# Expert weights split inside layer 0's loop, the experts' first norm on ScalarE, and the ranking behind an expert block

## The reference

```python
x = x + windowed_attention(group_norm(x))      # layer 0: 12 heads of 8, shifted 8x8 windows, q and k normalised
t = tokens(x)
t = t + local_attention(layer_norm(t))         # layer 1: 6 heads of 16, causal, 16 tokens back
scores = layer_norm(t) @ gate_w + gate_b       # 4 experts
probs  = softmax(scores); keep the top 2, divide by their sum
h = gelu(n @ w1[e] + b1[e])                    # 96 -> 384, n = layer_norm(t)
y = h @ w2[e] + b2[e]                          # 384 -> 96
t = t + sum over experts of gate[e] * y[e]
```

## Time and profile before

| | us |
|---|---|
| median of 3 runs (lowest, highest) | 498.88 (495.75, 503.75) |
| the profiled execution's own time | 497.59 |
| its span, first to last instruction | 493.5 |
| PE busy | 433.9 (88%) |
| DVE busy | 362.0 (73%) |
| ACT busy | 335.1 (68%) |
| POOL busy | 131.6 (27%) |

### The profile page before, as it was taken

The page is one execution under the profiler, slowest core; times in us unless marked ns, Lnnn a source line. Parts: engine busy times, 40 slices in busy tenths (PEclk is TensorE's granted clock), DMA queues, the critical chain, the costliest instruction groups (busy, mean ns, idle before and its releaser), DMA issues.

```text
span 493.5 us, 14736 instructions
## 1 busy us (share of the span) xinstructions
PE 433.9 (88%) x5354; PEld 324.2 (66%) x5354; DVE 362.0 (73%) x1056; ACT 335.1 (68%) x898; POOL 131.6 (27%) x257
## 2 busy tenths in 40 slices
PE   2547999999999996889999999788998999999995
PEld 1114767777776765667777777566885677777773
DVE  4976778787888788457767777647677777777776
ACT  1016787777778785268888888555777777777773
POOL 8302222222121226033433334553912000000000
PEclk9999999999999999589999999997999999999998
DMA  7112000000000000000000000000500232212300
GB/s 174 23 30 71 28 8 0 0 0 1 0 0 0 0 0 2 1 2 3 3 0 0 0 0 0 2 1 1 129 2 17 68 81 80 57 25 80 80 14 18
DMA packets 14326, 12.36 MB, mean 25 GB/s; under 512 B 12803, under 2 KB 13143, under 8 KB 13528
## 3 DMA queue, kind: packets, MB, share of 16 engines
q1 hardware_dynamic: 13128, 11.74, 9.3%
q10 hardware_dynamic: 1072, 0.08, 0.2%
q0 software_dynamic: 96, 0.14, 0.1%
HBM read 10.31 MB, written 1.70 MB: 24 GB/s over the span
## 4 chain that ended last, share of the span: by engine, by line
PE 65%; ACT 10%; DVE 10%; SPq 6%; issue 4%; DMA 2%; POOL 1%; DVEq 0%; ACTq 0%
PE bank L651 8%; PE bank L663 6%; PE score_banks L718 5%; PE score_banks L1283 4%; PE score_banks L1280 4%; PE score_banks L1281 4%; PE bank L684 3%; PE bank L708 3%; PE bank L590 3%; PE score_banks L1269 3%; PE score_banks L625 3%; PE score_banks L1270 3%; ACT probsT L816 3%; PE score_banks L1271 3%; PE score_banks L606 2%
## 5 line engine op out<-in xcount | busy, mean ns | idle before, releaser
L985 POOL TENSOR_TENSOR stack<-qk,ones 128x192 f16<-128x192 f32 x64 | 32.4, 506 | 183.2 <-DVE qk L907 115.4
L1432 DVE TENSOR_TENSOR hidden_lo<-hidden,hidden_hi 128x512 fp32r<-128x512 f32 x96 | 65.6, 685 | 20.1 <-ACT hidden_hi L1336 20.0
L839 DVE TENSOR_REDUCE negmax<-score_banks 128x12 bf16<-128x768 f32 (+1 forms) x64 | 48.2, 754 | 25.7 <-PE score_banks L625 25.7
L651 PEld LDWEIGHTS bank<-vals,probsT 128*64 128x64 f32 (+1 forms) x1536 | 36.9, 127 | 29.0 <-ACT probsT L813 19.1
L651 PE MATMUL bank<-vals,probsT 128*64 128x18 f32 (+1 forms) x1536 | 42.5, 208 | 13.9 <-ACT probsT L816 4.5
L1334 ACT ACTIVATE hidden<-score_banks 128x512 f32<-128x512 f32 x64 | 38.3, 598 | 21.7 <-PE score_banks L1271 17.7
L718 PE MATMUL score_banks<-perm,probs 128*128 128x128 f32 x288 | 43.9, 281 | 0.7 <-ACT probs L786 0.7
L663 PE MATMUL bank<-w_qkv,xnT 128*128 128x192 f32 x128 | 40.2, 398 | 3.9 <-DVE qk L907 3.0
L1280 PE MATMUL score_banks<-hidden_hi,w_hi 128*96 128x512 f32 x96 | 38.6, 402 | 2.2 <-ACT hidden_hi L1336 2.2
L1283 PE MATMUL score_banks<-hidden_lo,w_hi 128*96 128x512 f32 x96 | 38.5, 401 | 1.7 <-DVE hidden_lo L1432 1.7
L813 ACT ACTIVATE probsT<-score_banks 128x384 f32<-128x384 f32 x32 | 15.7, 490 | 34.4 <-PE score_banks L718 34.4
(11 more groups left out here) (195 smaller groups left out, 1105.5 us busy)
## 6 DMA issues: line engine op xcount, KB each, us to landing
xT_all<-gate_scratch SPq DMA_DIRECT2D x8, 768.0 KB, 5.2
x_all<-in_x SPq DMA_DIRECT2D x4, 384.0 KB, 7.3
out<-moe_final SPq DMA_DIRECT2D x8, 192.0 KB, 2.2
w<-in_w SPq DMA_DIRECT2D x1, 582.0 KB
w<-in_w SPq DMA_DIRECT2D x1, 576.0 KB
bias_f<-col_scratch SPq DMA_DIRECT2D x16, 24.0 KB
perm<-in_permutations SPq DMA_DIRECT2D x1, 320.0 KB, 3.2
w_qkv<-in_w_qkv SPq DMA_DIRECT2D x2, 109.1 KB
```

The lines of the kernel that those rows point to most:

```text
L651: last = pe.matmul(o_bank[rows, pair_of[h2] * 2 * vd:(pair_of[h2] + 1) * 2 * vd], probsT[:, h2, rows], buffer_of(k, odd, -1)[:, w, pair_of ...
L839: v.tensor_reduce(negmax[:].rearrange("p (g h) -> p g h", g=2), score_banks[k][:, :, 0:half].rearrange("p g (h j) -> p g h j", j=KEYS), AX ...
L1432: v.tensor_tensor(hidden_lo[m % HBUF][:], hidden[m % 2][:], hidden_hi[m % HBUF][:], ALU.subtract).then_inc(q["hidden_lo"], 1)
```

## The change

Four edits. First, w2_hi is made by ACT, between steps 2 and 3 of layer 0, behind a wait for `experts_loaded` at 64; POOL makes w1_lo and w2_lo in 24 slices each (64 and 48 columns wide), one pair at the end of each step of layer 0's loop; POOL's block of three operations after the loop is gone. Second, the guess of the experts' norm, part 0, is taken by ACT, between layer 1's loop and step N - 4, in place of POOL. Third, `dve_gates(0)` stands ahead of DVE's step N (the last division), no longer behind it, and `rank_first` stands in chunk 0, block 0, behind `dve_low`. Fourth, the statistics of part 1 move from ahead of the expert stage to chunk 0, block 2, behind `dve_low`; POOL's power of part 1 still waits for them.

```diff
@@ gpsimd
-            middle_steps(pool, a0["pool"])
+            pool.wait_ge(w1_split, 1)
+            pool.wait_ge(w2_split, 1)
+
+            def pool_middle(pool, b, k, odd):
+                a0["pool"](pool, b, k, odd)
+                split_weights(nc, s, q0, 2 * b + k)
+
+            middle_steps(pool, pool_middle)
             steps(pool, a0["pool"], N - 4, N - 2)
-            pool.wait_ge(w1_split, 1)
-            nc.gpsimd.tensor_tensor(s["w1_lo"][:], s["w1"][:], s["w1_hi"][:], ALU.subtract).then_inc(w1_split, 1)
-            pool.wait_ge(w1_split, 2)
-            pool.wait_ge(s["experts_loaded"], 16 * 4)
-            split_second_weights(pool, nc, s, q0["w2_split"])
+            pool.wait_ge(w1_split, 1 + MIDDLE)
+            pool.wait_ge(w2_split, 1 + MIDDLE)
             steps(pool, a1["pool"], -3, 4)
             middle_steps(pool, a1["pool"])
-            norm_power(pool, nc, s, qm, 0)
@@ vector
-            steps(v, a1["dve"], N, N + 1)
             moe["dve_gates"](v, 0)
-            moe["dve_rank"](v)
-            steps(v, a1["dve"], N + 1, N + 3)
-            norm_statistics(v, s, qm, 1, q1["stat_ready"])
-            moe["dve"](v)
+            steps(v, a1["dve"], N, N + 3)
+            moe["dve"](v, lambda: norm_statistics(v, s, qm, 1, q1["stat_ready"]))
@@ scalar
-            steps(act, a0["act"], 0, 4)
+            steps(act, a0["act"], 0, 3)
+            act.wait_ge(s["experts_loaded"], 16 * 4)
+            nc.scalar.activation(s["w2_hi"][:], s["w2"][:], ACT.Copy).then_inc(w2_split, 1)
+            steps(act, a0["act"], 3, 4)
             act.wait_ge(s["w1_loaded"], 16)
             nc.scalar.activation(s["w1_hi"][:], s["w1"][:], ACT.Copy).then_inc(w1_split, 1)
...
             middle_steps(act, a1["act"])
+            norm_guess(act, nc, s, qm, 0)
             steps(act, a1["act"], N - 4, N - 2)
+MIDDLE = UNITS - 8
+SLICE1, SLICE2 = EXPERTS * HID // MIDDLE, NH * C // MIDDLE
+
+def split_weights(nc, s, q, n):
+    one, two = bass.ds(SLICE1 * (n - 4), SLICE1), bass.ds(SLICE2 * (n - 4), SLICE2)
+    flat, hi, lo = (s[w][:].rearrange("p m c -> p (m c)") for w in ("w2", "w2_hi", "w2_lo"))
+    nc.gpsimd.tensor_tensor(s["w1_lo"][:, one], s["w1"][:, one], s["w1_hi"][:, one],
+                            ALU.subtract).then_inc(q["w1_split"], 1)
+    nc.gpsimd.tensor_tensor(lo[:, two], flat[:, two], hi[:, two], ALU.subtract).then_inc(q["w2_split"], 1)
@@ dve_chunk
             if is_chunk(c, 0):
                 if m == 0:
+                    rank_first(v)
                     dve_select(v, 0)
                     dve_renormalise(v, 0)
                 if m == 1:
                     dve_gates_T(v, 0)
+                if m == 2:
+                    last_statistics()
```

More of the change, by code:

```diff
@@ L1017, in whole_program @@
     N = UNITS
-    w1_split = q0["w1_split"]
+    w1_split, w2_split = q0["w1_split"], q0["w2_split"]
     with nc.Block() as block:
@@ L1464, in weigh_at, with dve_chunk @@
         return m // HC - 1 if m % HC == 1 and m > 1 else None
-    def dve_chunk(v, c, k):
+    def dve_chunk(v, c, k, last_statistics=None):
         for m in range(NH):
@@ L1559, in sync_program, with dve_program @@
             sp.wait_ge(stored[k], 16 * (CHUNKS // 2))
-    def dve_program(v):
-        chunks(v, dve_chunk)
+    def dve_program(v, last_statistics):
+        chunks(v, lambda v, c, k: dve_chunk(v, c, k, last_statistics))
         c, k = CHUNKS - 1, 1
@@ L1593, in experts @@
             "pe": pe_program, "pe_inputs": pe_inputs, "act_inputs": act_inputs, "dve_inputs": dve_inputs,
-            "pe_gates": pe_gates, "dve_gates": dve_gates, "dve_rank": rank_first,
+            "pe_gates": pe_gates, "dve_gates": dve_gates,
             "normalise": normalise_first}
```

## The result

The changed kernel takes 500.36 us (median of 20 runs, 496.65 to 502.37); the kernel before, run beside it, 497.01 (20 runs, 493.74 to 505.1). The ratio is 1.0072, 95% interval 1.0047 to 1.0097: a small loss, where a small gain was forecast. The profiled execution is the fastest of its 20: span 494.6, own time 496.65, mean granted clock 0.975 (before 493.5, 497.59, 0.969). It is 3.7 us under the kernel's median, while the profiled execution of the kernel before is 0.6 over the median of 497.01. So what follows takes places from the traces and the verdict from the timed runs; 4.3 us of what separates the two medians and the two profiled times is in neither trace.

What follows compares the result with a forecast made beforehand. PE was taken to set the pace in layer 0's loop, with stalls and half clock behind them at three places. Terms -8.5 + 0 + 7.0 - 3.3 + 1.2 = -3.6 gave 495.3 us; 8-in-10 range 487.5 to 503.5.

Steps and rivals of the forecast that it cites:

- Rival B: Layer 0 from 66 us: long half clock behind ACT's wait, 13.5 in place of 7, 501.8 us; chance 0.14.
- rival C: End of layer 0: clock falls all the same, gain 4 in place of 8.5, 499.8 us; chance 0.15.
- POOL's block at the end of layer 0: Removing it frees DVE's L962 and avoids PE's wait and half clock: -8.5 us, bounds 3 and 9.5.
- E: End of layer 0: DVE held by something other than POOL's block, no gain there, 503.8 us; chance 0.02.
- Slices: Layer 0's loop: they fall beside DVE's row maximum and cost 0 us, bounds 0 and 9.6.
- D: Layer 0's loop: slices catch DVE's root each step, +9.6 us, 504.9 us; chance 0.04.
- ScalarE's copy and wait: Ahead of layer 0's step 3: PE delayed 5.5 us, plus 1.7 of half clock; +7.0 taken, bounds 5 and 13.5.
- Rival A: Start of layer 0: ACT hardly waits for expert loads, cost 1 in place of 7, 489.3 us; chance 0.10.
- The guess by ScalarE: End of layer 1: DVE's 1.93 us idle for POOL's power goes, half clock too: -3.3 us, bounds 1.5 and 3.7.
- Gates, ranking, statistics: Expert stage: earlier gain eaten by PE waiting 2 to 3.6 us for chunk 4; +1.2 us, bounds -2.2 and +3.5.

Runs made afterwards that it cites:

- slices_only: Kernel before with the slices in layer 0's loop and GpSimd's w2 copy ahead of the loop, the rest as before; 489.73 us, ratio 0.9885.
- before_act_wait: Kernel before with only ScalarE's wait for the four expert loads and its w2 copy ahead of layer 0's step 3, replacing GpSimd's copy; 506.42 us, ratio 1.0179.
- stats_first: Changed kernel with part 1's statistics back ahead of the expert stage, ranking left behind the first block; 496.38 us, ratio 1.0017.
- before_guess: Kernel before with only the guess of the experts' norm made by ScalarE in place of GpSimd's power; 492.72 us, ratio 0.9916.
- before_order: Kernel before with only the new place of gates, ranking and part 1's statistics; 501.57 us, ratio 1.0075.
- both_stats0: Changed kernel with w1 issued last, w2 copied by GpSimd ahead of layer 0's loop, and part 1's statistics in block 0; 488.60 us, ratio 0.9828.
- swap_order: Kernel before with GpSimd's block at layer 0's end reordered: w2's copy and subtraction ahead of w1's subtraction; 492.33 us, ratio 0.9927.
- pool_copy: Changed kernel with w2_hi made by GpSimd between its step 3 and layer 0's loop, no expert-load wait on ScalarE; 489.59 us, ratio 0.9887.
- late_copy: Changed kernel with ScalarE's wait and w2 copy moved behind its w1 copy, ahead of layer 0's loop; 493.02 us, ratio 0.9948.
- w1_last_stats0: Changed kernel with w1 issued behind the other four expert loads and part 1's statistics in block 0 ahead of the ranking; 487.56 us, ratio 0.9849.
- w1_last: Changed kernel with SyncE issuing w1 behind the four small expert loads, ScalarE's wait left in place; 490.79 us, ratio 0.9904.

## Why the prediction was wrong

Every place was right, and so was the sign of every term that had one. The wait's term was too small, by the trace more than any other, and so the sum turned. The measured 500.36 still lies inside the range of 487.5 to 503.5, but only because that range took in rivals B and C; the forecast itself, 490 to 499 and a small gain, missed.

- POOL's block at the end of layer 0: -8.5 forecast, -8.40 in the traces of two kernels, -5.7 in the rounds of `slices_only`. "The larger part is the clock" is right. In the changed kernel the clock stayed full with PE busy four fifths, which was rival C's reason for a fall, so C and E are out there; the 3.4 us at half clock that five other versions show cost 0.8 and not C's 4.5. The size was taken from one execution, whose half-clock stretch of 17.1 us is the longer of the two lengths seen behind this stall.
- Slices: 0 forecast, 0.07 in `slices_only`. They take 0.32 and 0.28 us (0.38 and 0.35 estimated). The reason given holds: all 48 slices run beside VectorE's row maximum, some into the sum of squares (L884) behind it, and none beside the operations of the root (L896 to L902, four of them), which take 0.18 us each as before. So what a slice would do to the root was not met, and the rule quoted for D is neither borne out nor refuted here. In the changed kernel the loop's shift grows by 0.72, of which 0.63 fall in its first step, at the end of the half clock; D, at 9.6, is out.
- ScalarE's copy and wait: +7.0 forecast, +10.28 in the trace (with the 0.72), +8.9 in the rounds of `before_act_wait`. **This is the step that failed.** Its first half, how long PE stands still: 5.5 forecast, 6.64 measured (6.93 less the 0.29 of the earlier trace rows). Most of the 1.1 between them is the load. I took it as landed at 64.05, when before's last packet had gone, but ScalarE was released at 65.03, while no packet shows from 64.5 on, and the issue itself was 0.43 us later in this execution. So L776 came 7.3 us late and not 6.4. The rest is slack: I followed ScalarE's queue to the probabilities and let 0.9 us be absorbed, but VectorE stands in order too. Its copies of the probabilities and of `oT`, for which PE waits, are behind the sum of squares, and that waited 6.55 us for ScalarE's first instruction; 0.7 was absorbed. Its second half, the larger miss: the half clock. A stretch of 3.4 us was forecast, at 1.7; it lasted 13.7 us, and 3.6 of the 10.28 are left for it. Rival A is out. Rival B, the clock lasting, came nearest: 13.7 us of its 17, and a term just over the 10.1 from which it was to decide. Its price of 8 for the clock was too high, as PE stood still in 4.2 of the 13.7 us (63.7 to 67.89). `stats_first`, with 20.5 us there, came to 12.65 in all. Why the stretch lasts that long is not shown.
- The guess by ScalarE: -3.3 forecast, -3.28 in both traces, 0.84% or 4.2 us in the rounds of `before_guess`.
- Gates, ranking, statistics: +1.2 forecast, +2.08 in the trace, +1.93 and 0.75% or 3.7 us in `before_order`. The wait was foreseen and measured 2.39 (2 to 3.6 forecast), and so was the gain ahead of it (2.2 forecast, 2.07 measured). What the term left to its upper bound is the half clock behind the wait, 3.4 us at some 1.7.

The shifts add up: +0.14 ahead of the wait, +10.28, -8.40, -3.28 and +2.08 make +0.82, and +0.27 at the program's end the 1.09 by which the spans differ. The rounds add up as well: +1.79% for the wait, -1.15 for the slices, -0.84 for the guess and +0.75 for the order make +0.55%, beside 0.72 measured for all together (0.47 to 0.97). Against their forecasts the four are off by +1.9, +2.8, -0.9 and +2.5 us in the rounds, each with an interval of 2 to 3.4 us either way. In the traces the sum is off by 4.7 us (+1.1 in the span for -3.6): 3.3 of it at the start, 0.9 in the order, 0.5 in small parts at other places. That the gain at the end of layer 0 can be smaller than in before's profile is shown by two other traces; how often either length occurs is not.

## What to carry to other kernels

Ahead of a wait that is moved, look at when the last of its loads is issued and behind which bytes: a small load behind a large one that a single DMA engine works off is as late as the large one. Count the landing by what the load releases, and not by its last packet. Then follow the wait through every in-order queue and not only the engine that waits: the first consumer of its first instruction sets the length of the stall. And for a large operation that holds another engine, ask which instruction of that engine meets it: exchanging the order of two operations gave 6.15 us in the trace, where cutting the block in slices gave 8.4 (7.6 with the half clock behind it). Where a gain is mostly clock, read several executions: one profile can hold the long stretch.

## What the chip showed that was not expected

Stretches at 1.2 GHz behind a wait of PE differ in length, and the same wait has more than one: behind 3.27 us at the end of layer 0 there were 17.1 us (three profiles) or 6.8 (two); behind 6.9 at the start 13.7 us (two), behind 6.72 at the same place in `stats_first` 20.5; behind 2.05 in `both_stats0` 13.7, with PE busy in all 13.70 of them, behind 0.97 in `swap_order` 3.4. Behind the 1.3 us at the start of layer 1 five of twelve kernels show 3.4 us and seven none. What removes such a wait removes a cost that varies from execution to execution.

The program's own start varies as well. The same 24 matmuls of L651 (in one early step) take 0.88 us in the changed kernel at 51.96 and 1.48 in `pool_copy` at 53.09:

```profile
53.09 1.48 PE L651 MATMUL bank<-vals,probsT 128*64 128x18 f32 x24
60.66 1.16 PE L651 MATMUL bank<-vals,probsT 128*64 128x18 f32 x24
```

There the slow stage ends at about 61.7 us and not at 50. The granted clock reads 1.00 in both all the while, so only the durations show this stage. `qk` ahead of the changed code is 3.95 us late, which no edit of that version explains (`late_copy` 3.61, `w1_last_stats0` 4.79, `w1_last` 0.77). One profile's span is uncertain by that much. Differences between shifts on either side of a place are free of it, though not of the half-clock stretches at the place itself, as the 3 us at the end of layer 0 with nothing changed show.
